# First layer's attention: the other head's maxima products placed ahead of the exponential wait and the score products

## The reference

```python
q = _l2norm(q) * q_scale
k = _l2norm(k) * k_scale                        # 2 null keys stand ahead of the 2048 others
sim = jnp.einsum('bhid,bhjd->bhij', q, k) * ATTN_SCALE
sim = sim + dist[None, None] * slopes[None, :, None, None]
sim = jnp.where(causal_mask[None, None], neg, sim)
attn = jax.nn.softmax(sim, axis=-1)
out = jnp.einsum('bhij,bhjd->bhid', attn, v)
```

## Time and profile before

| | us |
|---|---|
| median of the runs | 2526.49 |
| the runs | 2523.24 to 2528.47 |
| span of the profiled execution | 2534.2 |
| busy TensorE matmul / weight load | 2097.0 / 978.8 |
| busy VectorE / ScalarE / GpSimd | 1323.7 / 919.7 / 917.7 |
| mean granted TensorE clock | 0.886 |

### The profile page before, as it was taken

The page is one execution under the profiler, slowest core; times in us unless marked ns, Lnnn a source line. Parts: engine busy times, 40 slices in busy tenths (PEclk is TensorE's granted clock), DMA queues, the critical chain, the costliest instruction groups (busy, mean ns, idle before and its releaser), DMA issues. The chain is left out here.

```text
span 2534.2 us, 36034 instructions
## 1 busy us (share of the span) xinstructions
PE 2097.0 (83%) x11003; PEld 978.8 (39%) x11003; DVE 1323.7 (52%) x2796; ACT 919.7 (36%) x1323; POOL 917.7 (36%) x775
## 2 busy tenths in 40 slices
PE   1586389989899898998989994379679999999998
PEld 1254134334344334333343332256334334344433
DVE  6134474464654547455474416612456576566674
ACT  0112034444343443434434450223134444434454
POOL 1404465575555665556565672700310000000000
PEclk9798589999899999999999995589769899779898
DMA  3121401111011110111101101333200000000000
GB/s 126 46 80 42 89 6 31 36 31 31 6 31 38 31 37 0 31 36 30 36 0 31 33 1 45 109 91 102 59 9 30 30 1 29 30 1 29 29 2 17
DMA packets 68494, 93.32 MB, mean 37 GB/s; under 512 B 19486, under 2 KB 48306, under 8 KB 67430
## 3 DMA queue, kind: packets, MB, share of 16 engines
q1 hardware_dynamic: 64230, 82.97, 12.1%
q0 software_dynamic: 4096, 8.40, 1.2%
HBM read 37.91 MB, written 19.60 MB: 23 GB/s over the span
## 5 line engine op out<-in xcount | busy, mean ns | idle before, releaser
L1303 POOL TENSOR_TENSOR a_prob_sum<-a_prob_sum,a_prob 128x512 f32<-128x512 f32 (+3 forms) x512 | 563.1, 1100 | 338.3 <-ACT a_prob L1250 314.5
L1250 ACT ACTIVATE a_prob<-a_ps_st,a_table 128x512 f32<-128x512 f32 (+3 forms) x640 | 390.0, 623 | 631.4 <-PE a_ps_st L1114 348.8
L1378 DVE TENSOR_REDUCE a_maxima<-a_ps_mx 128x1 f32<-128x512 f32 (+5 forms) x704 | 371.4, 563 | 306.0 <-PE a_ps_mx L1091 188.3
L1683 DVE TENSOR_REDUCE a_maxima<-a_mx 128x1 f32<-128x512 f32 (+3 forms) x640 | 362.5, 606 | 195.3 <-PE a_mx L1673 111.5
L1942 ACT ACTIVATE a_prob<-a_st 128x1024 f32<-128x1024 f32 (+1 forms) x320 | 293.4, 938 | 386.5 <-PE a_st L1843 189.3
L1138 PE MATMUL a_ps_ot<-a_prob,a_values 128*64 128x512 f32 (+3 forms) x1280 | 334.8, 583 | 0.0
L1091 PE MATMUL a_ps_mx<-a_k_ext,a_q_max 128*128 128x512 f16 (+5 forms) x704 | 217.5, 355 | 116.6 <-DVE a_maxima L1378 53.8
L1673 PE MATMUL a_mx<-a_ks,a_qs 72*128 72x512 bf16 (+3 forms) x640 | 246.5, 394 | 41.1 <-DVE a_maxima L1683 27.9
L1843 PE MATMUL a_st<-a_qs,a_ks 97*128 97x512 bf16 (+1 forms) x640 | 242.3, 398 | 8.2 <-issue 4.3
L1113 PE MATMUL a_ps_st<-a_q_both,a_k_both 128*128 128x512 f16 (+3 forms) x640 | 231.1, 361 | 3.6 <-ACT a_null_p L1242 3.6
L1114 PE MATMUL a_ps_st<-a_q_rest,a_k_ext 128*128 128x512 f16 (+3 forms) x640 | 227.0, 357 | 0.0
(11 more groups left out here) (228 smaller groups left out, 2656.7 us busy)
## 6 DMA issues: line engine op xcount, KB each, us to landing
a_q_both<-a_q_hi SPq DMA_DIRECT2D x32, 256.0 KB
f_w<-in_w SPq DMA_DIRECT2D x28, 256.0 KB, 2.8
expert_in<-zeros SPq DMA_DIRECT2D x5, 1024.0 KB, 10.7
a_qs<-parts SPq DMA_DIRECT2D x48, 96.0 KB
a_ks<-parts SPq DMA_DIRECT2D x48, 96.0 KB
a_k_ext<-a_k_hi SPq DMA_DIRECT2D x16, 256.0 KB
a_q_max<-a_q_hi SPq DMA_DIRECT2D x16, 256.0 KB
a_k_both<-a_k_hi SPq DMA_DIRECT2D x16, 256.0 KB
```

The source lines that it names most:

```text
L1250: act.activation(prob[:, n % NPROB, c0:QW], bank[:, c0:QW], ACT.Exp, bias=table[x][:, at:at + 1]).then_inc(exp_done, 1)
L1303: pool.tensor_tensor(into[:, c0:QW], into[:, c0:QW], prob[:, n % NPROB, c0:QW], ALU.add).then_inc(added, 1)
L1378: dve.reduce_max(maxima[:, qt, n:n + 1], ps_mx[c % 2][:, 0:z - a], AX_X).then_inc(mx_done, 1)
L1683: dve.reduce_max(own.maxima[:, NT * a + qt, n:n + 1], own.ps_mx[nth % 2][:, 0:hi - lo], AX_X).then_inc(own.mx_done, 1)
```

## The change

In each slot TensorE's maxima products, with their waits, come ahead of the wait for the exponential and of the score products. The units and the weighted sums keep their place behind both. In slots without maxima products (0 to 7, 34 to 40) nothing is different. The other engines' programs are unchanged.

```diff
--- before.py
+++ after.py
@@ -1150,14 +1150,14 @@
                         pe.wait_ge(head_loaded[x], i * (16 * HEAD_LOADS) + 16 * HEAD_LOADS)
                         pe.wait_ge(v_copied, 2 * i + x + 1)
                         pe.wait_ge(row_loaded, i * 32 + 16 * x + 16)
-                    if NB0 * x + b >= 2 or not first:
-                        pe.wait_ge(exp_done, i * (2 * NB0) + NB0 * x + b - 1)
-                    scores(x, b)
                     for c in maxes:
                         if c == 0:
                             pe.wait_ge(head_loaded[1 - x], (i + x) * (16 * HEAD_LOADS) + 16 * HEAD_LOADS)
                         chunk(1 - x, c, NC0 + i * (2 * NC0) + chunks - 1)
                         chunks += 1
+                    if NB0 * x + b >= 2 or not first:
+                        pe.wait_ge(exp_done, i * (2 * NB0) + NB0 * x + b - 1)
+                    scores(x, b)
                     for kind, n in units:
                         free = base + done - 1
                         bank = (MISC_FIRST + done) % 2
```

## The result

The changed kernel takes 2544.8 us (median of 20 runs, 2525.8 to 2565.4) beside 2527.8 us of the kernel before on the same chip (20 runs, 2518.2 to 2547.8). The ratio is 1.0054, interval 1.0029 to 1.0079: between 7 and 20 us slower, 13.6 us in the middle. (The ratio leaves out the one run of the 20 that fell into a slower state, with a lower clock, and isn't the quotient of the two medians, which lie 17.0 us apart.) The forecast was 2532.6 in a range of 2523 to 2545. So the sign was right, and the size is at the very end of the range, 0.2 us inside it.

The account below looks back on a forecast made before the run. TensorE's instruction order was taken to set the time; second heads and the eighth pair's first head 0.9, first heads at slot 8 0.2, other first-head terms 5.0: 2526.5 + 6.1 = 2532.6 us, range 2523 to 2545.

Parts of the forecast that it names:

- What bounds the stage: First layer's attention: TensorE's instruction order sets the time, busy 269.69 us of 300; next to nothing to win at the exponential's wait.
- Rival (a): Odd slots: the 0.10 us score weight load gets hidden, 19.5 us faster, 2507; chance 7%.
- Slot 8 of second heads, idle time: TensorE's wait for the head's loads grows from 2.80 to 3.24 us, lag +0.44 in 7 heads.
- The giving back in diagonal slots: Second heads, slots 12, 22 and 24: shorter score products shrink the lag by 0.11 us each, 0.33 per head.
- First heads: Seven first heads with projections: lag of 0.7 us per head, 5.0 us in all, bounds 0 to 10.
- M(15): Slot 15's maxima products in first heads: half the VectorE chain hangs on slot 13's projection, +0.2 us (0 to 0.44).
- M(20): Slot 20's maxima products in first heads: can't come earlier, VectorE being packed; +0.44 us, wait growing from 0.60 to 1.0.
- slots 30 to 32: First heads with projections: slot 30's exponential starts 0.27 us later and the next transpose follows, +0.27 per head.
- The clock: Behind slot 8 of second heads: the sum counted the longer wait as +0.44 us of lag, with no added clock cost.
- Rival (b): Longer waits at slots 20, 31 and 8: four to six more clock falls add 8 to 12 us, 2541 to 2545; 20%.
- the transpose of slot 31: Sign in the profile after: this transpose, which waited 0.77 us before, would wait 1.0 us.
- the null block's exponential: Slots 0 to 2: score products' wait for it, 3.6 us in 4 events, would be unchanged, out of the change's reach.

Follow-up runs that it names:

- the second execution: Second profiled execution of the changed kernel, from its repeat without edit beside the kernel before: 2543.0 us, ratio 1.0041 (1.0007 to 1.0076).

## Why the prediction was right, and where it was wrong

**What bounds the stage** was right: TensorE's order, and nothing to win at the exponential's wait. The 0.81 us of idle weight load was rightly read as covered. Rival (a) is out.

**Slot 8 of second heads, idle time.** Right in size: the wait is 3.30 for 2.80, with +0.44 of lag in each of 7 heads. **The giving back in diagonal slots** was right as well, and somewhat low: -0.33 per head was worked out, -2.9 / 7 = -0.42 measured. Order alone leaves 3.1 - 2.9 = 0.2 us in the second heads; the sum had 0.8 in these seven.

**First heads.** The sum had +5.0 us. Slots 10 to 22 measured +7.5 in seven heads that have projections, 1.07 each, where 0.44 + 0.2 was worked out. Both terms are mis-sized. At M(15) I gave the chain half of the 0.44, and it took the whole and more, a wait of 1.36 for 0.72: +0.58 from slot 14 to 16, of which slots 16 to 18 give back 0.25, so +0.33 for +0.2. Slots 18 to 20 cost +0.65 for +0.44. The mechanism there is the one foretold, VectorE packed since a unit started it, but the new wait is M(19)'s 0.78 and M(20)'s stays at 0.60: the lag arises one slot earlier than I put it. Between full-clock starts slots 28 to 30 (+0.13 to +0.27), slots 30 to 32 (+0.15, for +0.27) and 34 to 36 (+0.08, for -0.2) cost little. What slots 26 to 28 do, where I had the lag kept, isn't settled: at full clock they take 6.13 and 7.03 us in the two heads before that show it and 6.15 after. Slots 10 to 22 and 30 to 36, the ones that repeat, make +8.5 us for +5.0. M(28)'s wait shrank from 1.81 to 1.53.

**The clock** is the step that failed. The sum let the +0.44 us of slot 8 count as +0.44. Rival (b) had the right mechanism and the wrong place and count: four to six more falls in 14 heads, from waits growing to 1.0 us and that of slot 8. In the traces the waits of 0.6 to 1.4 us in slots 10 to 22 of first heads are followed by hardly any low clock (0 us in sum before, 0.3 after). It is a fall that was there before in each second head which lasts longer: 32 us at low clock became 64, about 15 us lost by the table's first row (17.9) less 3.1. I had looked at one second head, in a 10 us stretch whose 0.87 shows that slot 8 already paid the clock, and took it as a constant. The Trainium skill, "TensorE: Matmul & The Clock Gate", section "Loop structure matters more than you think", puts the clock at half when a long wait for a DMA, 8 us in its example, stands between the matmuls. Here waits of some 3 us do it, and with the wait filled the clock stays up (1.00 for 0.87); the 1.36 us wait at M(15) doesn't show it.

The parts that repeat make more than the whole: 17.9 - 2.9 + 7.5 + 1.0 = 23.5 us, against 7 to 20 by the runs (the other rows take back some 3 us, to 20.6 in the profiled stage). Of these the order is 3.1 - 2.9 + 8.5 = 8.7 us. By the runs that leaves 13.6 - 8.7 = 5 us for the clock (-2 to 11), by the profiled executions 15. How much the clock costs in a typical run is therefore open between these; that it costs is shown by the experiments that fill the wait.

The value 2532.6 came 12.2 us short. Beside the kernel before on the same chip it is +13.6 for +6.1: 2.6 us of that are order (8.7 for 6.1), and 5 are left for the clock. The range held because rival (b), wrongly placed, had been priced in, and by luck: 0.2 us more and the median was outside.

Of the signs named for the profile after, three came: the wait for the load near 3.2 us (3.30), the transpose of slot 31 near 1.0 (0.92), and more waiting for maxima in sum (+2.7 for +4). M(20) at 1.0 did not, and the null block's exponential, which was to stay at 3.6 us, was waited for 2.7 us in 3 events (3.2 in 4 in the second execution).

## What to carry to other kernels

In this kernel a long wait of the engine that sets the time cost twice: its length, and the slow clock on the dense work behind it. So before anything is moved past such a wait, read the granted clock in equal stretches behind every occurrence of it, not behind one; and look for work that can be moved into it, which here (the weighted sums of slot 8, ready at that point) brought 2%, while moving work out of it cost 0.5% in the whole change and 1.5% on its own. The waits of 0.6 to 1.4 us in slots 10 to 22 had no such price and could be costed by their length. That isn't a rule for all waits under 2 us: in first heads of the kernel before the clock fell right behind the 1.4 to 1.7 us waits of slot 8 (with 0.3 to 0.65 us for the weights after them), and behind those of slots 27 and 28, which follow each other closely:

```profile
685.17 0.34 PE L1091 MATMUL a_ps_mx<-a_k_ext,a_q_max 128*128 128x384 f16 x1 [1.25 <-DVE a_maxima L1378]
...
687.81 0.34 PE L1091 MATMUL a_ps_mx<-a_k_ext,a_q_max 128*128 128x386 f16 x1 [1.81 <-DVE a_maxima L1378]
```

From slot 22 to 30 the clock was low for 34 us in first heads, which no change here went after.

## What the hardware showed that I had not expected

- The clock stayed at 1.2 GHz for up to 12 us of full work behind a wait of 3.1 to 3.5 us (0.62 over 18 us with TensorE busy 15.2).
- Products that nobody needs, 84 score products of 0.22 us in the whole run, made the kernel 1.2% faster.
- TensorE stands still at the start of the loop in some rounds, with no releaser that the profile shows, and the clock is low behind it in most of them. Doubled score products in the loop go with more such rounds, 4 or 5 of 6 for 0 to 2:

```profile
950.22 0.63 PE L1106 MATMUL a_ps_st<-a_q_both,a_null_k 128*32 128x512 f16 x4 [4.07 <-issue]
```

- The runs of one kernel lie up to 40 us apart, and their mean clocks go with it: of the changed kernel's, one of 2523.2 us had 0.894 and one of 2552.2 us 0.876.
